# An attention block's warm-up in another order: gate matrices loaded in the prologue, first queries placed by two engines

## Chip, cores, metric

One core of a Trainium2 chip. The metric is the device time of one launch in microseconds, median of some runs; lower is better.

## The reference

A transformer block with modulation (adaLN), float32, x of 2 x 1024 x 512:

```
mod = silu(c) @ wmod                       # c 2x512, wmod 512x3072: shift, scale, gate, twice
sa, ca, ga, sb, cb, gb = mod               # gates: sign(g) * max(|g|, 0.25)
h = layernorm(x) * (1 + ca) + sa
x = x + ga * attention(h, Wq, Wk, Wv, Wo)  # 32 query heads, 8 key heads, width 64, rotary, causal
h = layernorm(x) * (1 + cb) + sb
x = x + gb * ffn(h)                        # ternary weights, silu gate, rms norm, hidden 2048
```

## The kernel before

Each engine's instructions are written out by hand; semaphores order them across engines. There are four parts: a prologue, attention, the output projection and the feed-forward part. The change is in the first two.

**Names.** TensorE is PE, VectorE DVE, ScalarE ACT, GpSimd POOL, SyncE SP. Float32 products are made of a high part (float32r) and a low part, so most tiles come in two: `hT_hi` and `hT_lo` hold the modulated, turned x, `w_hi` and `w_lo` the weights of one group (4 query heads, 1 key head, 1 value head).

**Prologue** (`prologue`). SP issues the loads: c, the first shift and scale matrices (1 MB each), x in four quarters of 512 rows, weights of group 0, rotary tables, and the second ("late") shift and scale matrices into `vectors.late[0]`. The first two quarters of x are normalised on DVE into tiles `xn`, which lie in `p_32` (`rows_at`), a tile that attention uses only later; the place for the gate matrices, `vectors.late[1]`, overlaps them. The first quarter is turned by PE and modulated by ACT. A barrier of all engines ends the prologue.

**Attention** runs in steps T = 0 to 71 for each of 8 groups g, every engine through the same `step(body, T)`. What an engine does in a step is found from tables: `body.uses(T, delay)` gives the projections that started `delay` steps ago, `body.before(T, at)` is true once, in the warm-up. The warm-up is group -1, steps 28 to 71, and does what group 0 needs before its first step. Its projections (`X_USES`) start at steps 31 and 36 (keys, with values on the upper partitions), 42 (values turned), 44, 49 (`qx`, first and last quarter of the queries' columns, two heads each), 54, 59 (`qy`, the middle quarters) and 68 (first keys of the next batch half).

A projection takes PE four steps. Then, counted from its start: at 4 DVE multiplies it with cosines and sines into `rot_c` and `rot_s` (L951, L952), which frees PSUM bank `X_BANK` for the next projection; at 5 SP swaps halves of `rot_s` into `rot_x` by DMA (L608; two transfers for keys, four for queries); at 6 POOL adds (L1051); at 8 ACT splits off the high part (queries: L907, keys: L903, at 12 in the warm-up); POOL makes the low part (queries: L1062 at 8, keys: L1056); at 10 SP places queries into `q_hl` by four DMAs (L620). There are two buffers of `rot_*`; a buffer is reused only when its placing has landed (`await_buffer`).

**Late rows and products.** The other quarters of x (n = 1, 2, 3) are finished in the warm-up: statistics (L160), square root on ACT, normalisation (L81 to L85, then four L175 into `late.xn`), PE turns (L182), ACT modulates (L853, L854, twice for each of four pieces), DVE makes the low part (L973). The first scores wait for all of ACT's modulations (`late.h_ready`), since the turns use the banks of the scores. `late_product(v)` multiplies silu(c) with the late shift, late scale and the two gate matrices (v = 0 to 3; L118, eight matrix instructions each) at steps 35, 41, 64, 66, in banks 4 and 5. The first waits for `late.h_ready` of quarter 1, because ACT still reads those banks. The gate matrices are loaded by SP at step 50. DVE makes the gates out of the last two products at steps 67 to 71, and SP stores them by eight small DMAs at step 71 (L661).

**Scores** of group 0's first rows are at steps 63 to 70 of the warm-up; DVE takes maxima (L934), ACT exponentials (L844), whose table ACT loads before the first.

Of the kernel before, what the change touches and what calls it, by code (L numbers as in the profile page):

```python
# [27 lines left out]
P = 128  # L28
B, S, E = 2, 1024, 512
T = B * S  # L30
# [62 lines left out]
class Vectors:  # L93


    def __init__(self, nc, ctx, p_32):
        sem = lambda n: ctx.enter_context(nc.semaphore("a_" + n))
        self.cs = ctx.enter_context(nc.sbuf_tensor("cs", [P, B * CT], F32))
        flat = p_32[:].rearrange("p a h c -> p (a h c)")
        size = CT * 2 * E  # L100
        self.late = [flat[:, at:at + size].rearrange("p (k v e) -> p k v e", k=CT, v=2) for at in (0, 2 * GQ * 9 * P - size)]
        self.flat = flat
# [5 lines left out]
    def rows_at(self, n):  # L108
        size = 4 * E
        return self.flat[:, (2 + n) * size:(3 + n) * size].rearrange("p (t e) -> p t e", t=4)  # L110

# [4 lines left out]
    def product(self, pe, out, wm, v):  # L116
        for kc in range(CT):
# [19 lines left out]
class LateRows:  # L137
# [11 lines left out]
    def place(self, nc, ctx):  # L149

        sb = lambda n, s: ctx.enter_context(nc.sbuf_tensor(n, s, F32))
        self.xt = sb("xt_l", [P, 2, 4, E])
        self.xn = sb("xn_l", [P, 2 * P_RING, 512])[:, 0:4, :]
        self.h32 = [sb("h32_l%d" % n, [P, 2, 512]) for n in range(2)]
# [52 lines left out]
def prologue(nc, ps, x, c, wmod, ident_in, ident, modT, hT_hi, hT_lo, vectors, late, load_first, load_tables, w_in, w_raw,  # L207
             w_hi, w_lo, k_scaled, whi_ready, w_ready):
    with ExitStack() as ctx:
# [6 lines left out]
        xt, xn = [x_rows[:, n] for n in range(2)], [vectors.rows_at(n) for n in range(2)]  # L216
# [12 lines left out]
        def _(sp):  # L229
# [14 lines left out]
            for v, place in enumerate((SHIFT[1], SCALE[1])):  # L244
                sp.dma_start(vectors.late[0][:, :, v, :], wm_v[:, :, place, :]).then_inc(vectors.late_in, 16)
            load_x(3, late.xt[:, 1])
# [135 lines left out]
def attention(nc, ps, wq, wk, wv, w_gu, w_p, consts_in, w_in, w_raw, cos, sin, mask, ident, hT_hi, hT_lo, ot_dram, rden_dram,  # L382
              tern_gu, tern_p, o_sb, o_out, load_first_weights,
              w_hi, w_lo, p_32, k_scaled, whi_ready, w_ready, vectors, late, modT, gates_dram, wmod, spare):
    with ExitStack() as ctx:
# [201 lines left out]
        def late_h32(n, k):  # L587

            return spare[:, k // 2, k % 2, :] if n == 1 else late.h32[k // 2][:, k % 2, :]


        @block.sync
        def _(sp):
# [17 lines left out]
            def place(g, n):  # L611

                kind, unit, hp, _ = X_USES[n]
                buf = buf_of(n)
                if g < 0 and kind == "qx":
                    sp.wait_ge(late.xn_ready, 3 + hp)
                q_low[buf].await_(sp, g, QBUF[buf].index(n))
                for h in range(2):
                    for at, src in ((half[0], rot_s), (half[1], rot_x)):
                        sp.dma_start(as_f32(quarters(q_hl[at, 2 * hp + h, :], kind)),  # L620
                                     src[half[h], buf, :].rearrange("p (q c) -> p q c", q=2)).then_inc(q_placed[buf], 16)

# [13 lines left out]
            def step(body, T):  # L636
                places_first = body.before(T, QUERY_SWAP)
                if places_first:
                    for g, n, _ in body.uses(T, 10, kinds=("qx", "qy")):
                        place(g, n)  # L640
                for g, n, _ in body.uses(T, 5, kinds=("kv", "qx", "qy")):
                    swap(g, n)
                if not places_first:
                    for g, n, _ in body.uses(T, 10, kinds=("qx", "qy")):
                        place(g, n)
# [28 lines left out]
        def _(pe):  # L674
# [91 lines left out]
            def late_turns(n):  # L766
                for k in range(CT):
                    if k == 0 or n == 3:
                        pe.wait_ge(late.h_ready, 2 * CT + (k + 1 if n == 3 else 0))
                    late.turn(pe, n, k, ps[:, turned_bank(n, k), :], late.xn, ident)  # L770

            def late_product(v):
                if v == 0:
                    pe.wait_ge(vectors.late_in, 32)
                    pe.wait_ge(late.h_ready, 2 * CT)
                if v >= 2:
                    pe.wait_ge(vectors.gate_in, 32)
                    pe.wait_ge(vectors.late_rows, v - 1)
                vectors.product(pe, ps[0:B, T_BANK + v % 2, :], vectors.late[v // 2], v % 2).then_inc(vectors.late_done, 1)

            def step(body, T):
# [3 lines left out]
                for v in range(4):  # L785
                    if body.before(T, LATE_AT[v]):
                        late_product(v)
# [23 lines left out]
        def _(act):  # L811
# [44 lines left out]
            def step(body, T):  # L856
# [6 lines left out]
                if body.before(T, CONSTS_AT):  # L863
                    act.wait_ge(consts_in, 48)
                    act.copy(ident_b[:], ident[:]).then_inc(consts_ready, 1)
                    act.copy(mask_b[:], mask[:]).then_inc(consts_ready, 1)
                for v in range(2):
                    if body.before(T, LATE_ROWS[v]):
                        act.wait_ge(vectors.late_done, v + 1)
                        act.copy(rd_all[0:B, v, :], ps[0:B, T_BANK + v, :]).then_inc(vectors.late_rows, 1)  # L870
# [33 lines left out]
                for g, n, _ in body.uses(T, 8, kinds=("qx", "qy")):  # L904
# [129 lines left out]
        def _(pool):  # L1034
# [4 lines left out]
            def step(body, T):  # L1039
# [18 lines left out]
                for g, n, _ in body.uses(T, 8, kinds=("qx", "qy")):  # L1058
# [727 lines left out]
```

## Time and profile before

| | |
|---|---|
| median of 3 runs | 1859.02 us (1857.18 to 1862.01) |
| profiled execution | 1858.29 us |
| its span | 1856.3 us |
| TensorE busy | 1747.3 us, 94% |
| VectorE, ScalarE, GpSimd busy | 68%, 62%, 52% |
| mean granted TensorE clock | 0.987 |

Busy shares are of the whole span. Times below are microseconds from the start of the span. In a timeline row the first number is the start and the second the length; a bracket at the end gives the idle time before the instruction and what ended it. `x4` means four instructions merged, and the length is then from the first's start to the last's end. Instructions of ScalarE and TensorE overlap their neighbours a little.

### The profile page before, as it was taken

To read this page: it belongs to the slowest core of one execution; us is meant where nothing else is said; L and a number is where in the kernel's file an instruction comes from. 1 tells how busy PE (TensorE), PEld (TensorE's weight loads), DVE (VectorE), ACT (ScalarE), POOL (GpSimd) and SP (SyncE) were. 2 spreads that over 40 slices of the span, in tenths; PEclk is the share of its full clock that TensorE was granted. 3 is DMA by queue.
4 is the path that set the end of the run, shared out by engine and by line. 5 is a ranking of instruction groups with operands and counts; after the bars stand their busy time and mean duration, and the time that the engine had idled before them with its cause. 6 is when DMAs were issued, how large, how long until landed. Compare 5 with 4: busy or idle time off the path is not lost. (4 is left out here: it accounts for less than half of the span.)

```text
span 1856.3 us, 28089 instructions
## 1 busy us (share of the span) xinstructions
PE 1747.3 (94%) x9505; PEld 1394.7 (75%) x9505; DVE 1259.0 (68%) x2078; ACT 1147.6 (62%) x2315; POOL 964.8 (52%) x773
## 2 busy tenths in 40 slices
PE   6899999999999999999999999996999999999998
PEld 3577787777777777778777777774788778888886
DVE  5787887788788778788778878884333355545343
ACT  4578787777777777877777777784322354323322
POOL 1256667666667666666766666753000035444454
PEclk9999999999999999999999999998999999999999
DMA  6433444344344344344434434425655400101000
GB/s 229 121 94 103 120 102 124 100 109 121 88 131 114 86 123 112 92 117 108 121 103 108 125 83 134 119 82 163 208 179 177 134 29 1 52 1 51 1 29 23
DMA packets 174969, 190.95 MB, mean 103 GB/s; under 512 B 31456, under 2 KB 117736, under 8 KB 174832
## 3 DMA queue, kind: packets, MB, share of 16 engines
q1 hardware_dynamic: 137840, 140.99, 26.7%
q10 hardware_dynamic: 36992, 48.25, 9.4%
q8 instruction: 72, 1.18, 0.3%
q14 instruction: 65, 0.53, 0.1%
HBM read 86.12 MB, written 31.74 MB: 63 GB/s over the span
## 5 line engine op out<-in xcount | busy, mean ns | idle before, releaser
L926 DVE TENSOR_TENSOR p_lo<-ps_b,p_hi 128x512 fp32r<-128x512 f32 x576 | 395.3, 686 | 194.7 <-ACT p_hi L829 190.8
L844 ACT ACTIVATE p<-ps_b,negm 128x640 f32<-128x640 f32 (+7 forms) x512 | 381.9, 749 | 111.4 <-DVE negm L934 108.5
L829 ACT CAST p_hi<-ps_b 128x512 fp32r<-128x512 f32 x576 | 337.0, 588 | 156.9 <-PE ps_b L748 154.2
L934 DVE TENSOR_REDUCE negm<-ps_b 128x1 f32<-128x640 f32 (+7 forms) x512 | 375.8, 744 | 34.1 <-PE ps_b L738 33.4
L748 PE MATMUL ps_b<-ident,p 128*128 128x128 f32 x2304 | 350.3, 275 | 3.1 <-DVE p_lo L926 2.1
L736 PE MATMUL ps_b<-k_hh,q_hl 128*128 128x512 f32 (+3 forms) x768 | 270.1, 352 | 37.0 <-ACT p L844 36.0
L762 PE MATMUL ps_b<-p_hi,v_hl 128*128 128x512 f32 x576 | 276.9, 481 | 16.4 <-ACT o_sb L837 16.1
L748 PEld LDWEIGHTS ps_b<-ident,p 128*128 128x128 f32 x2304 | 259.0, 141 | 37.3 <-DVE p_lo L926 5.1
L737 PE MATMUL ps_b<-k_l,q_hl 128*128 128x512 f32 (+3 forms) x768 | 256.1, 346 | 0.0
L763 PE MATMUL ps_b<-p_lo,v_hl 128*128 128x512 f32 x576 | 227.6, 395 | 0.0
L736 PEld LDWEIGHTS ps_b<-k_hh,q_hl 128*128 128x128 f32 x768 | 145.1, 189 | 87.4 <-ACT p L844 54.7
L1492 PE MATMUL ps_d<-h_hi,gu 128*128 128x512 f32 x512 | 201.0, 393 | 1.1 <-DVE h_lo L1612 1.1
L1493 PE MATMUL ps_d<-h_lo,gu 128*128 128x512 f32 x512 | 200.2, 391 | 0.0
L1042 POOL TENSOR_TENSOR o_sb<-o_sb,o_low 64x512 f32<-64x512 f32 x128 | 176.3, 1382 | 33.4 <-DMA o_low<-o_sb 33.4
L1051 POOL TENSOR_TENSOR rot_c<-rot_c,rot_x 128x512 f32<-128x512 f32 (+1 forms) x96 | 124.9, 1301 | 105.9 <-DMA rot_x<-rot_s 105.2
L700 PE MATMUL ps_b<-hT_hi,w_hi 128*128 128x512 f32 x384 | 160.4, 418 | 8.6 <-DVE rot_s L952 5.1
L1062 POOL TENSOR_TENSOR rot_x<-rot_c,rot_s 128x512 fp32r<-128x512 f32 x64 | 83.0, 1297 | 163.0 <-ACT rot_s L907 163.0
L737 PEld LDWEIGHTS ps_b<-k_l,q_hl 128*128 128x128 f32 x768 | 145.0, 189 | 27.9
L1047 POOL TENSOR_TENSOR o_sb<-o_sb,rd_all 64x512 f32<-64x512 f32 x128 | 163.4, 1281 | 3.9
L1588 POOL TENSOR_TENSOR sq<-a 128x512 f32<-128x512 f32 x60 | 71.2, 1186 | 163.9 <-DVE a L1662 163.4
L701 PE MATMUL ps_b<-hT_hi,w_lo 128*128 128x512 f32 x384 | 152.4, 397 | 0.0
L702 PE MATMUL ps_b<-hT_lo,w_hi 128*128 128x512 f32 x384 | 151.4, 394 | 0.0
(156 smaller groups left out, 3202.6 us busy)
## 6 DMA issues: line engine op xcount, KB each, us to landing
rot_x<-rot_s SPq DMA_DIRECT2D x320, 64.0 KB, 2.0
q_hl<-rot_s SPq DMA_DIRECT2D x128, 128.0 KB, 2.5
q_hl<-rot_x SPq DMA_DIRECT2D x128, 128.0 KB, 2.5
rd_all<-reciprocals SPq DMA_DIRECT2D x128, 128.0 KB, 3.0
o_low<-o_sb ACTq DMA_DIRECT2D x128, 128.0 KB, 2.4
attention_out<-o_sb SPq DMA_DIRECT2D x128, 128.0 KB, 2.5
o_raw<-attention_out SPq DMA_DIRECT2D x32, 512.0 KB, 4.9
wf<-in_L_ffn_w_gate_up ACTq DMA_DIRECT2D x32, 256.0 KB, 3.0
```

Of the source, the lines that this page charges most:

```text
L736: pe.matmul(ps[:, bank, 0:n], q, k_hh[unit][:, k0:k0 + n], start=True, stop=False)
L737: ins = pe.matmul(ps[:, bank, 0:n], q, k_l0[:, unit, k0:k0 + n], start=False, stop=(k0 + n < nk))
L748: ins = pe.transpose(ps[:, T_BANK + T % 2, h * P:(h + 1) * P], p_32[:, parity, h, column * P:(column + 1) * P], ident[:])
L762: pe.matmul(ps[:, O_BANK, :], v_hl[unit][:, j, :], p_hi[:, T % P_RING, :], start=(j == 0), stop=False)
L763: pe.matmul(ps[:, O_BANK, :], v_hl[unit][:, j, :], p_lo[:, T % P_RING, :], start=False, stop=(j == i)).then_inc(pv_done, 1)
L829: act.copy(p_hi[:, T % P_RING, :], ps[:, T_BANK + T % 2, :]).then_inc(phi_ready, 1)
L844: act.activation(p_32[:, parity, h, column * P:column * P + nk], s, ACT.Exp, bias=negm[:, k:k + 1], scale=1.0, accum_out=den[:, parity, k: ...
L926: dve.tensor_tensor(p_lo[:, T % P_RING, :], ps[:, T_BANK + T % 2, :], p_hi[:, T % P_RING, :].bitcast(F32), ALU.subtract).then_inc(plo_read ...
L934: dve.tensor_reduce(negm[:, k:k + 1], s, AX.X, ALU.max, negate=True).then_inc(max_ready, 1)
L1042: pool.tensor_tensor(o_sb[0:D, n % 2, :], o_sb[0:D, n % 2, :], o_low[:, n % 2, :], ALU.add).then_inc(o_added, 1)
L1492: pe.matmul(ps[:, bank + half, :], gu[:, m, half, k, :], h_hi[:, parity, k, :], start=(k == 0), stop=False)
L1493: i = pe.matmul(ps[:, bank + half, :], gu[:, m, half, k, :], h_lo[:, parity, k, :], start=False, stop=(k == CT - 1))
```

## The change

- `xn` of the first two quarters moves out of `p_32` into `late.h32` (now one tile) and `late.xn`. The gate matrices' place is then free in the prologue, and SP loads them there, ahead of the last quarter of x; the load at step 50 goes.
- The late products use banks 2, 3, 4, 5 and v = 0 waits for its matrices only. The second is cut in two halves, at steps 41 and 43. The turns of quarter 2 wait until ACT has copied the products out of banks 2 and 3.
- The low parts of the last two pieces of quarter 1 move from steps 33 and 34 to 36, behind the first rotation; statistics of quarter 2 from 36 to 37, its root from 41 to 38.
- `place` takes an engine and a list of heads. In the warm-up SP places head 0 of each `qx` pair at delay 10 and ACT head 1 at delay 9 (steps 53 and 58).
- In the warm-up the `qy` splits on ACT and POOL move from delay 8 to 12, their placing from 10 to 12.
- The constants' casts move from step 52 to 58, and a small exponential at step 59 has ACT load that table there.

```diff
-        xt, xn = [x_rows[:, n] for n in range(2)], [vectors.rows_at(n) for n in range(2)]
+        xt, xn = [x_rows[:, n] for n in range(2)], [late.h32, late.xn]
...
                 sp.dma_start(vectors.late[0][:, :, v, :], wm_v[:, :, place, :]).then_inc(vectors.late_in, 16)
+            vectors.load_gates(sp, wmod)
             load_x(3, late.xt[:, 1])
...
-LATE_AT, LATE_TURN, LATE_ROWS = (35, 41, 64, 66), 70, (45, 45)
-GATE_LOAD, GATE_STEPS, GATE_STORE = 50, 67, 71
-ROWS_STAT, ROWS_ROOT, ROWS_NORM, ROWS_TURN = (36, 49), (41, 50), (44, 54), (48, 58)
+LATE_AT = ((35, 0, (0, 1, 2, 3)), (41, 1, (0, 1)), (43, 1, (2, 3)), (64, 2, (0, 1, 2, 3)), (66, 3, (0, 1, 2, 3)))
+LATE_BANK, LATE_ROWS, LATE_TURN = (2, 3, T_BANK, T_BANK + 1), (45, 45), 70
+GATE_STEPS, GATE_STORE = 67, 71
+ROWS_STAT, ROWS_ROOT, ROWS_NORM, ROWS_TURN = (37, 49), (38, 50), (44, 54), (48, 58)
-ROWS_LOW = ((31, 32, 33, 34), (55, 55, 56, 56), (59, 60, 61, 62))
-CONSTS_AT, KEYS_AT, QUERY_SWAP = 52, 12, 59
+ROWS_LOW = ((31, 32, 36, 36), (55, 55, 56, 56), (59, 60, 61, 62))
+CONSTS_AT, KEYS_AT, QUERIES_AT, QUERY_SWAP, TABLE_AT = 58, 12, 12, 59, 59
...
+        def place(eng, g, n, heads):
+            kind, unit, hp, _ = X_USES[n]
+            buf = buf_of(n)
+            if g < 0 and kind == "qx":
+                eng.wait_ge(late.xn_ready, 3 + hp)
+            q_low[buf].await_(eng, g, QBUF[buf].index(n))
+            for h in heads:
+                for at, src in ((half[0], rot_s), (half[1], rot_x)):
+                    eng.dma_start(as_f32(quarters(q_hl[at, 2 * hp + h, :], kind)),
+                                  src[half[h], buf, :].rearrange("p (q c) -> p q c", q=2)).then_inc(q_placed[buf], 16)
...
+                    for g, n, _ in body.uses(T, 10, kinds=("qx",)):
+                        place(sp, g, n, (0,) if g < 0 else (0, 1))
+                for g, n, _ in body.uses(T, QUERIES_AT if body.g < 0 else 10, kinds=("qy",)):
+                    place(sp, g, n, (0, 1))
-                if body.before(T, GATE_LOAD):
-                    sp.wait_ge(vectors.late_done, 2)
-                    vectors.load_gates(sp, wmod)
...
+                    if k == 0 and n == 2:
+                        pe.wait_ge(vectors.late_rows, 2)
-            def late_product(v):
+            def late_product(v, pieces):
                 if v == 0:
                     pe.wait_ge(vectors.late_in, 32)
-                    pe.wait_ge(late.h_ready, 2 * CT)
-                if v >= 2:
+                if v >= 2 and 0 in pieces:
                     pe.wait_ge(vectors.gate_in, 32)
-                    pe.wait_ge(vectors.late_rows, v - 1)
...
+                if body.g < 0:
+                    for g, n, _ in body.uses(T, 9, kinds=("qx",)):
+                        place(act, g, n, (1,))
+                if body.before(T, TABLE_AT):
+                    act.activation(den[:, 1, :], ident[:, 0:len(ROWS)], ACT.Exp)
...
-                for g, n, _ in body.uses(T, 8, kinds=("qx", "qy")):
+                for g, n, _ in body.uses(T, 8, kinds=("qx",)) + body.uses(T, QUERIES_AT if body.g < 0 else 8, kinds=("qy",)):
```

## Rows read from the trace of the kernel before

**Rows 1.** Windows: stretch, its length, busy us by engine, clock, DMA share.
```profile
27.00:92.00 65.00, 52.55 (x218) 31.48 (x219) 43.87 (x79) 33.95 (x63) 18.05 (x14) 0.95 0.36 105
92.00:290.00 198.00, 190.21 (x1132) 153.47 (x1131) 161.57 (x272) 153.15 (x334) 125.96 (x102) 1.00 0.40 106
```

**Rows 2.** Timeline of TensorE, first key projection: start, length, line, instruction, idle.
```profile
29.75 0.39 PE L702 MATMUL ps_b<-hT_lo,w_hi 128*128 128x512 f32 x1
32.71 3.59 PE L118 MATMUL ps_b<-p,cs 128*2 128x512 f32 x8 [2.58 <-ACT hT_hi L854]
```

**Rows 3.** Timeline of VectorE, same stretch and the step after.
```profile
32.60 0.69 DVE L973 TENSOR_TENSOR hT_lo<-wo_raw,hT_hi 128x512 fp32r<-128x512 f32 x1 [0.65 <-ACT hT_hi L854]
...
45.47 1.13 DVE L85 TENSOR_TENSOR rstd<-rstd,tmp 128x4 f32<-128x4 f32 x1
```

**Rows 4.** Timeline of all engines around the value rows.
```profile
43.20 1.26 POOL L1051 TENSOR_TENSOR rot_c<-rot_c,rot_x 64x512 f32<-64x512 f32 x1 [3.88 <-DMA rot_x<-rot_s]
...
44.81 0.50 PE L700 MATMUL ps_b<-hT_hi,w_hi 128*128 128x512 f32 x1 [1.40 <-DVE v_hl L996]
...
45.27 1.31 POOL L1056 TENSOR_TENSOR k_l<-rot_c,k_hh 64x512 fp32r<-64x512 f32 x1 [0.80 <-ACT k_hh L903]
...
46.63 2.88 DVE L175 TENSOR_SCALAR xn_l<-xt_l,mv,rstd 128x512 f32<-128x512 f32 x4
```

**Rows 5.** Page, DMA issues: tiles, count, size, us to landing.
```profile
rot_x<-rot_s SPq DMA_DIRECT2D x320, 64.0 KB, 2.0
```

**Rows 6.** Timeline of SyncE, 52 to 104 us.
```profile
53.29 1.16 SPq L114 DMA_DIRECT2D p<-in_L_wmod  x2
55.80 2.42 SPq L608 DMA_DIRECT2D rot_x<-rot_s  x4
...
61.44 0.61 SPq L620 DMA_DIRECT2D q_hl<-rot_x  x1
...
91.25 1.19 SPq L608 DMA_DIRECT2D rot_x<-rot_s  x2
```

**Rows 7.** Timeline of all engines, first two groups of queries.
```profile
62.70 1.26 POOL L1051 TENSOR_TENSOR rot_c<-rot_c,rot_x 128x512 f32<-128x512 f32 x1 [3.40 <-DMA rot_x<-rot_s]
63.93 0.69 DVE L951 TENSOR_TENSOR rot_c<-ps_b,cos 128x512 f32<-128x512 f32 x1 [1.95 <-DMA q_hl<-rot_x]
63.99 0.62 ACT L907 CAST rot_s<-rot_c 128x512 fp32r<-128x512 f32 x1 [6.35 <-POOL rot_c L1051]
...
64.69 1.28 POOL L1062 TENSOR_TENSOR rot_x<-rot_c,rot_s 128x512 fp32r<-128x512 f32 x1 [0.73 <-ACT rot_s L907]
...
69.17 0.81 ACT L854 ACTIVATE hT_hi<-ps_b,modT 128x512 fp32r<-128x512 f32 x1
...
70.50 0.47 PE L736 MATMUL ps_b<-k_hh,q_hl 128*128 128x512 f32 x1 [0.63 <-DMA q_hl<-rot_x]
```

**Rows 8.** Timeline of ScalarE, the table load.
```profile
74.58 1.28 ACT L844 ACT_TABLE_LOAD   x1
75.88 1.11 ACT L844 ACTIVATE p<-ps_b,negm 128x1024 f32<-128x1024 f32 x1
...
89.31 0.19 ACT L844 ACTIVATION_READ_ACCUMULATOR p<-ps_b,negm 128x1 f32 x1
```

**Rows 9.** Timeline of ScalarE, first steps of group 0.
```profile
98.56 1.25 ACT L903 CAST k_hh<-rot_c 64x512 fp32r<-64x512 f32 x2
```

**Rows 10.** Timeline of TensorE at its next wait.
```profile
102.09 0.39 PE L736 MATMUL ps_b<-k_hh,q_hl 128*128 128x256 f32 x1 [0.97 <-ACT p L844]
```

**Rows 11.** Windows as in Rows 1.
```profile
66.00:69.00 3.00, 3.00 (x9) 2.27 (x9) 1.71 (x3) 3.00 (x5) 0.00 (x0) 0.53 0.48 114
```

**Rows 12.** Timeline of SyncE, prologue.
```profile
14.44 0.43 SPq L235 DMA_DIRECT2D xt_l<-in_L_attn_x  x1
...
16.61 2.27 SPq L235 DMA_DIRECT2D xt_l<-in_L_attn_x  x1
```

**Rows 13.** Waits of SyncE, 15 to 28 us: total, times, longest.
```profile
SPq L209 <- PEq L209: 8.0, 1, 8.0
```

More of the change, by code:

```diff
@@ L114, in load_gates, with product @@
             sp.dma_start(self.late[1][:, :, v, :], mod_columns(wmod)[:, :, GATE[v], :]).then_inc(self.gate_in, 16)
-    def product(self, pe, out, wm, v):
-        for kc in range(CT):
+    def product(self, pe, out, wm, v, pieces=range(CT)):
+        for kc in pieces:
             i = pe.matmul(out, self.cs[:].rearrange("p (b k) -> p k b", b=B)[:, kc, :], wm[:, kc, v, :],
@@ L153, in place @@
         self.xn = sb("xn_l", [P, 2 * P_RING, 512])[:, 0:4, :]
-        self.h32 = [sb("h32_l%d" % n, [P, 2, 512]) for n in range(2)]
+        self.h32 = sb("h32_l", [P, CT, 512])
     def statistics(self, dve, n, xt):
@@ L587, in late_h32 @@
         def late_h32(n, k):
-            return spare[:, k // 2, k % 2, :] if n == 1 else late.h32[k // 2][:, k % 2, :]
+            return spare[:, k // 2, k % 2, :] if n == 1 else late.h32[:, k, :]
+        def place(eng, g, n, heads):
[8 more added lines that the diff above has]
+                                  src[half[h], buf, :].rearrange("p (q c) -> p q c", q=2)).then_inc(q_placed[buf], 16)
         @block.sync
@@ L609, in swap @@
                                  rot_s[32 * (i ^ 1):32 * (i ^ 1) + 32, buf, :]).then_inc(swapped[buf], 16)
[L611 to L621, printed above, removed]
             def save_den(g, n):
@@ L643, in step @@
                 if not places_first:
-                    for g, n, _ in body.uses(T, 10, kinds=("qx", "qy")):
-                        place(g, n)
+                    for g, n, _ in body.uses(T, 10, kinds=("qx",)):
+                        place(sp, g, n, (0,) if g < 0 else (0, 1))
+                for g, n, _ in body.uses(T, QUERIES_AT if body.g < 0 else 10, kinds=("qy",)):
+                    place(sp, g, n, (0, 1))
                 for g, n in body.pairs(T, 2):
@@ L769, in late_turns @@
                         pe.wait_ge(late.h_ready, 2 * CT + (k + 1 if n == 3 else 0))
+                    if k == 0 and n == 2:
+                        pe.wait_ge(vectors.late_rows, 2)
                     late.turn(pe, n, k, ps[:, turned_bank(n, k), :], late.xn, ident)
-            def late_product(v):
+            def late_product(v, pieces):
                 if v == 0:
                     pe.wait_ge(vectors.late_in, 32)
-                    pe.wait_ge(late.h_ready, 2 * CT)
-                if v >= 2:
+                if v >= 2 and 0 in pieces:
                     pe.wait_ge(vectors.gate_in, 32)
-                    pe.wait_ge(vectors.late_rows, v - 1)
-                vectors.product(pe, ps[0:B, T_BANK + v % 2, :], vectors.late[v // 2], v % 2).then_inc(vectors.late_done, 1)
+                i = vectors.product(pe, ps[0:B, LATE_BANK[v], :], vectors.late[v // 2], v % 2, pieces)
+                if CT - 1 in pieces:
+                    i.then_inc(vectors.late_done, 1)
             def step(body, T):
@@ L784, in step @@
                         late_turns(n)
-                for v in range(4):
-                    if body.before(T, LATE_AT[v]):
-                        late_product(v)
+                for at, v, pieces in LATE_AT:
+                    if body.before(T, at):
+                        late_product(v, pieces)
                 if body.before(T, LATE_TURN):
@@ L869, in step @@
                         act.wait_ge(vectors.late_done, v + 1)
-                        act.copy(rd_all[0:B, v, :], ps[0:B, T_BANK + v, :]).then_inc(vectors.late_rows, 1)
+                        act.copy(rd_all[0:B, v, :], ps[0:B, LATE_BANK[v], :]).then_inc(vectors.late_rows, 1)
                 if body.before(T, LATE_TURN + 1):
@@ L1057, in step @@
                                        k_hh[unit][0:D, kv_cols(part)].bitcast(F32), ALU.subtract).then_inc(k_ready, 1)
-                for g, n, _ in body.uses(T, 8, kinds=("qx", "qy")):
+                for g, n, _ in body.uses(T, 8, kinds=("qx",)) + body.uses(T, QUERIES_AT if body.g < 0 else 8, kinds=("qy",)):
                     buf = buf_of(n)
```

6 lines of the change are left out of this document (removed).

## Prediction

> **What bounds the kernel now.** I read the windows first. In group 0 (92 to 290 us) TensorE is busy 190.2 of 198 us; in the stretch after the prologue (27 to 92 us) only 52.6 of 65 [rows 1]. The change touches nothing after that stretch but the order in which its leftovers are finished, so 12.4 us of idle TensorE is all there is to win, and a microsecond saved before 92 moves everything after it, since the groups are bound by TensorE. Next I read the timeline of that stretch engine by engine and, at each gap of TensorE, asked who released it. There are four gaps that matter.
>
> First, TensorE ends the first key projection at 30.14 and stands until 32.71, because the product of the late shift matrix waits for ScalarE's last modulation of rows 512 to 1023 [rows 2]. Second, after the value rows it waits for VectorE's low part and starts the first queries at 44.81; VectorE then normalises the third quarter of x until 46.63 + 2.88 = 49.51 and can only then rotate those queries [rows 4]. Third, between 53 and 64 the queries go round SyncE, GpSimd and ScalarE. The gate matrices, 2 MB, are issued at 53.29, ahead of the four swaps of the second queries (55.80); the sum that needs those swaps starts at 62.70 [rows 6, 7]. The median swap lands in 2.0 us [rows 5], so the last, issued near 57.6, would have been in at 59.7: the gates cost 3.0 us. Fourth, the scores start at 70.50, when both the last placed query and ScalarE's last modulation (69.17 + 0.81 = 69.98) are there [rows 7]. After that TensorE is nearly always busy.
>
> **The change, part by part.** I work in the old trace's times and sum the shifts.
>
> *Late products.* The shift product moves to another bank and no longer waits for ScalarE: it starts at 30.2 instead of 32.71, -2.5 us [rows 2]. The second key projection behind it also needs the low parts of that quarter. These end at 32.60 + 0.69 = 33.3 [rows 3], also when the last two go behind the first rotation; the product itself ends at 33.7, so it hides them. Of the scale product only half now stands ahead of the value rows; that is 3.59 / 2 = 1.8 us more [rows 2]. The other half runs while ScalarE and VectorE split the values, a wait TensorE has anyway. VectorE's value split thus ends at 44.75 - 4.3 = 40.5.
>
> *What is late next.* VectorE's normalisation. Of its old 4.8 us (44.75 to 49.51), L85 took 1.13 us, although it has four columns; it started at 45.47 and ended with GpSimd's L1056 (45.27 to 46.58). The four L175 behind it took 2.88 [rows 3, 4]; the second L1056 lay in them. I take about 1.9 us of the 4.8 as waiting for GpSimd. The key sum that GpSimd did at 43.20 [rows 4] now comes at 40.7 and the two key splits behind it, so the normalisation meets three of GpSimd's operations instead of two. Without any blocking it takes 2.9 us, but TensorE's query projection then ends near 44.0 and sets the rotation: -5.5. With all three in series (3 x 1.3) it takes 6.8 us: -2.2. I take one more partial wait, 5.8 us, ending 46.3: **-3.2 us**.
>
> The page "SBUF — State Buffer" of the Trainium skill, section "SBUF: two separate sides", calls the port that VectorE and GpSimd share "an exclusive lock, not a bandwidth split". The trace agrees (1.13 us for four columns). By that rule alone the three operations are all paid, and this term is -2.2.
>
> *Gates in the prologue.* Two issues go in ahead of the last load of x, which moves behind them. That load took 2.27 us to issue against 0.43 for the one before [rows 12], so issuing is already held up by the queue; two more at 2.27 end SyncE's prologue 4.5 us later. SyncE waited 8.0 us there [rows 13], which covers it. Above 4 us an issue it would not. The last quarter of x is read only near 50 us, far behind. Cost nothing; it takes away the 3.0 us delay of the second queries' swaps.
>
> *First two groups of queries.* Four placements of 0.61 us each are now split, two on SyncE, two on ScalarE; the last starts 1.2 us sooner. For the first queries this brings the third queries' rotation (63.93, held by the placing [rows 7]) forward by 1 to 2 us. But the chain that ends last goes on through ScalarE: second sum 59.7 to 61.0; split high 0.62, to 61.6; GpSimd's low split 1.28, to 62.95; ScalarE waits for this since its own placing now stands in its queue, then issues twice 0.61, to 64.2. Behind that instruction stand the four modulations of the last quarter, for which the first scores wait. They started right behind the cast of 63.99 (at about 64.5), and now at 64.2. So the 3.0 us are nearly eaten by the wait and the issues. The two small casts of constants fall in the wait for GpSimd and cost nothing; without that cover they cost under 1 us.
>
> *Table load.* It is taken from 74.58, where it held no TensorE work (the next score rows were issued meanwhile), and put between the first and second of these modulations: 1.28 us [rows 8] and some 0.2 for its small exponential. Nothing covers it there. The modulations end at 69.98 - 0.3 + 1.5 = 71.2, and the scores start at 71.2 instead of 70.50: **+0.7 us**.
>
> The page "ScalarE: Activation LUTs" of the Trainium skill, section "What ACT_TABLE_LOAD costs", gives about 1380 ns of drain on top of the load. The trace shows none: the activation starts 0.02 us behind the load. By that page the term would be +2.1.
>
> *TensorE's clock.* The fourth projection of queries now ends near 66.4 and TensorE idles until 71.2, 4.8 us. In the old trace it idled until 65.27 and in 66 to 69 us the granted clock was 0.53, the lower level of 1.2 GHz [rows 11]. That low stretch hid behind ScalarE; after 71.2 it would not. Half of 3 us is 1.5; none if the clock has risen by then. I take **+0.75**.
>
> *Third and fourth groups later.* Their splits and placements move four steps back. For the third this is free: placed before its buffer is next rotated. The fourth is now split by ScalarE behind the last warm-up exponential (ends 89.50 [rows 8]): to 90.1; GpSimd 1.28, to 91.45; SyncE places four times 0.65, to 94.05. Behind this stand the gate stores (2.4 us, until now ended at 91.2) and then the swaps of the next keys, issued at 91.25 before [rows 6] and now at 96.4. These keys are then summed from about 99.1 to 100.4. ScalarE copies them at 98.56 [rows 9] and would wait 1.8 us, with exponentials behind it; TensorE's next wait there is for just such an exponential [rows 10]. Between nothing (if ScalarE's slack takes it) and 1.9, nearer the row of a wait that is there already: **+1.5**.
>
> Sum: -3.2 + 0.7 + 0.75 + 1.5 = -0.25 us on the profiled execution's 1858.29 (1856.3 of span and 2.0 around it), so 1858.0. The median is 0.7 above that execution: 1858.8. What measurement tells from no change is 0.3%, 5.6 us.
>
> **Rivals.**
> - *Gains stand.* VectorE hardly meets GpSimd (-5.5), scores +0.7, no low clock, ScalarE's slack absorbs the late keys: -4.8, 1854.2. For it: 12.4 us of idle are there. Against: both extra waits are in plain sight. 0.20; with other small gains it passes 5.6 us in a third of these.
> - *The early gain stays with VectorE's waits.* All three of GpSimd's operations are paid in full, so the first term is -2.2, the others as above: 1859.8. For it: L85 waited for the whole rest of L1056; against: only one of the four L175 was longer, so not every operation meets one. 0.15. This is what the lock of the page "SBUF — State Buffer" would do.
> - *Slower by the clock.* After 4.8 us of idle the clock stays at 1.2 GHz through the two gate products (3.6 us each at full clock) and the score rows among them: 7.2 us and up to 2 more. It decides once the low stretch behind 71 us is over 6 us long; the one in the trace is about 3. -3.2 + 0.7 + 1.5 + 8 = +7: 1866. 0.08.
> - *The load drains.* The load holds ScalarE 1.4 us longer than its row: 1860.2. It would be a mechanism of ScalarE finishing its pending modulation before the load; a cast ends at 74.56 and the load starts at 74.58, with no such gap. The page is that of the ScalarE tables named above. 0.07.
> - *The forecast*, 1858.8, its own range 1856 to 1862: 0.50.
>
> **How the numbers follow.** All but the ends of two cases lie within 5.6 us. Faster: a third of 0.20 and a little of the others, 0.08. Slower: the clock, 0.08. Same: 0.84. For 8 in 10 the range takes in the gains case (1854.2) and the drain, and leaves out the clock case: 1853.8 to 1863.4. Its terms reach -5.5 + 0.7 at one end, and -2.2 + 2.1 + 1.5 + 1.9 = +3.3 at the other, with a microsecond for the scatter of medians.
>
> **What would show it.** In the profile after: the first late product of TensorE near 30.2; the value rows near 38.5; L175 of the third quarter ending near 46.3 (43.5 or 47.2 for the bounds); the swaps of the second queries landing 2 us behind their issue; a load of tables between two modulations; the first scores near 68.0; a clock row under 1 behind them; a ScalarE wait for GpSimd's key sum near 97 us. I am wrong if the first scores start before 66 or if TensorE shows no new idle time near 100 us, or if the gain is lost in the prologue, which should end at 27.1 as now.

## The result and the profile after

| | before | after |
|---|---|---|
| median of 12 runs | 1858.96 us | 1867.56 us |
| lowest, highest | 1855.43, 1865.49 | 1859.09, 1871.47 |
| profiled execution, span | 1858.29, 1856.3 | 1866.66, 1864.7 |
| mean granted clock | 0.987 | 0.985 |

The medians lie 8.6 us apart. The ratio, estimated from all runs, is 1.0038, 95% interval 1.0025 to 1.0050: slower by 0.38%, some 7 us (4.6 to 9.3). The forecast was 1858.8 with a range up to 1863.4 and 0.84 on "no change"; slower had 0.08.

Windows of the changed kernel, columns as in the rows before. The first two answer to [rows 1]:

```profile
27.00:92.00 65.00, 49.22 (x186) 28.21 (x186) 40.30 (x71) 30.65 (x52) 18.07 (x13) 0.87 0.30 93
92.00:290.00 198.00, 189.07 (x1110) 152.69 (x1109) 158.38 (x269) 151.77 (x333) 119.27 (x96) 0.98 0.39 103
```

TensorE did 186 instructions up to 92 us where it had done 218, at a mean clock of 0.87 instead of 0.95. To see where the time goes I measured how far each turn of probabilities in group 0 (the four transposes that open a step; L748 before, L745 after) starts behind the same one before. This is worked out from the timelines of TensorE, start minus start:

| mark | before | after | lag |
|---|---|---|---|
| first scores | 70.50 | 73.79 | +3.29 |
| turn of step 0 | 88.58 | 93.98 | +5.40 |
| step 5 | 98.53 | 103.93 | +5.40 |
| step 11 | 110.43 | 119.86 | +9.43 |
| step 0 of group 1 | 238.06 | 247.47 | +9.41 |
| last of group 7 | 1268.17 | 1277.13 | +8.96 |

All is lost in three places before 120 us: 3.3 us before the scores, 2.1 between them and step 0, 4.0 between steps 5 and 11. Then the lag stays.

The timeline of TensorE after, in the same form as [rows 2, 4, 7, 10]:

```profile
31.52 3.60 PE L113 MATMUL ps_b<-p,cs 128*2 128x512 f32 x8
...
42.27 0.50 PE L697 MATMUL ps_b<-hT_hi,w_hi 128*128 128x512 f32 x1
...
47.75 3.49 PE L177 MATMUL ps_b<-ident,xn_l 128*128 128x128 f32 x16 [2.44 <-DVE xn_l L170]
...
73.79 0.80 PE L733 MATMUL ps_b<-k_hh,q_hl 128*128 128x512 f32 x1 [7.96 <-ACT hT_hi L853]
...
75.92 4.73 PE L113 MATMUL ps_b<-p,cs 128*2 128x512 f32 x8
...
108.63 0.39 PE L733 MATMUL ps_b<-k_hh,q_hl 128*128 128x256 f32 x1 [2.11 <-ACT p L843]
```

The late product waits for nothing any more and the first queries start at 42.27 instead of 44.81. But then there is an idle stretch of 2.44 us and one of 7.96, and each time the row behind it is long: sixteen turns take 3.49 us (1.94 before), the gate product 4.73 (3.60). The clock was low in four places up to 120 us. These are the windows that TensorE worked in (the third low stretch began at 68.0, in the idle time):

```profile
27.00:30.40 3.40, 3.39 (x8) 2.72 (x9) 1.29 (x2) 3.40 (x6) 1.92 (x2) 0.51 1.05 410
47.50:50.90 3.40, 3.15 (x15) 3.19 (x16) 3.40 (x7) 2.03 (x4) 0.00 (x0) 0.50 0.15 37
73.80:78.20 4.40, 4.40 (x8) 1.65 (x9) 3.08 (x4) 0.91 (x1) 0.00 (x0) 0.50 0.13 34
109.00:115.80 6.80, 6.80 (x32) 5.54 (x31) 4.43 (x9) 3.98 (x13) 2.32 (x2) 0.50 0.09 21
```

All four are near 0.5, the lower level of 1.2 GHz, and TensorE works there nearly without a break. Each begins behind or in an idle stretch of more than 2 us: 2.96, 2.44, 7.96 and 2.11. The first of the four lies on the first key projection, which is why the late product starts at 31.52 and not near 30.2. The kernel before had its low stretches at 21.8 to 25.2, 45.7 to 49.1 and 66.2 to 69.6 us, the second 0.9 us behind an idle stretch of only 1.40 us; and it had none behind one of 2.58 us, before 32.71. So idle time alone does not tell where the clock falls.

The way to the first scores, on the timeline of the other engines (to be held against [rows 7]):

```profile
57.96 0.70 SPq L599 DMA_DIRECT2D q_hl<-rot_s  x1
...
59.06 2.49 DVE L977 TENSOR_TENSOR hT_lo<-h_l,hT_hi 128x512 fp32r<-128x512 f32 x4
...
59.65 3.03 POOL L1055 TENSOR_TENSOR rot_c<-rot_c,rot_x 128x512 f32<-128x512 f32 x1 [3.07 <-DMA rot_x<-rot_s]
...
62.71 0.62 ACT L911 CAST rot_s<-rot_c 128x512 fp32r<-128x512 f32 x1 [7.50 <-POOL rot_c L1055]
...
64.80 0.62 ACTq L599 DMA_DIRECT2D q_hl<-rot_s  x1
...
65.44 0.87 ACTq L599 DMA_DIRECT2D q_hl<-rot_x  x1
...
66.75 0.78 ACT L852 ACTIVATE h_l<-ps_b,modT 128x512 f32<-128x512 f32 x1 [3.02 <-issue]
...
68.22 1.28 ACT L870 ACT_TABLE_LOAD   x1
```

The swaps of the second queries are in by 59.65, 3 us earlier than at 62.70. GpSimd's sum then takes 3.03 us instead of 1.26: it lies over VectorE's four low parts. ScalarE casts at 62.71, and its first modulation comes 4.0 us later, at 66.75; before, it came 0.5 us behind the cast. The load of the table adds 1.5.

The third place, on the timelines of SyncE and ScalarE (against [rows 6, 9]):

```profile
98.55 2.52 SPq L658 DMA_DIRECT2D gates<-o_sb  x8
101.12 1.19 SPq L618 DMA_DIRECT2D rot_x<-rot_s  x2
```

```profile
105.10 1.26 ACT L907 CAST k_hh<-rot_c 64x512 fp32r<-64x512 f32 x2 [1.21 <-POOL rot_c L1055]
```

The next keys' swaps, 2.7 us behind the turn of step 0 before, are 7.1 us behind it now, and ScalarE waits for their sum.

### The profile page after: what moved, and what is told of

The parts are those of the page before. It is cut to its first block and busy times, and to the rows that moved or that the text cites. A ratio compares the mean times of both kernels' runs of the same rounds, so it can differ in the third digit from the quotient of the medians.

```text
span 1864.7 us, 28089 instructions
## 1 busy us (share of the span) xinstructions
PE 1748.5 (94%) x9505; PEld 1395.1 (75%) x9505; DVE 1261.1 (68%) x2078; ACT 1148.7 (62%) x2316; POOL 966.2 (52%) x773
## 5 line engine op out<-in xcount | busy, mean ns | idle before, releaser
L745 PE MATMUL ps_b<-ident,p 128*128 128x128 f32 x2304 | 351.1, 275 | 3.1 <-DVE p_lo L930 2.1
L745 PEld LDWEIGHTS ps_b<-ident,p 128*128 128x128 f32 x2304 | 259.7, 142 | 37.4 <-DVE p_lo L930 5.2
L1055 POOL TENSOR_TENSOR rot_c<-rot_c,rot_x 128x512 f32<-128x512 f32 (+1 forms) x96 | 130.1, 1356 | 116.0 <-DMA rot_x<-rot_s 115.8
L1046 POOL TENSOR_TENSOR o_sb<-o_sb,o_low 64x512 f32<-64x512 f32 x128 | 173.1, 1357 | 32.9 <-DMA o_low<-o_sb 32.8
```

Of the source, the lines that this page charges most:

```text
L745: ins = pe.transpose(ps[:, T_BANK + T % 2, h * P:(h + 1) * P], p_32[:, parity, h, column * P:(column + 1) * P], ident[:])
L1046: pool.tensor_tensor(o_sb[0:D, n % 2, :], o_sb[0:D, n % 2, :], o_low[:, n % 2, :], ALU.add).then_inc(o_added, 1)
```

## The experiments

My theory after the profiles: ScalarE's placing and the late splits of the third and fourth groups cost the most, and idle stretches cost again by the clock. The rivals are with each run. The baseline is run again beside each group of four; its median was 1858.8, 1858.0 and 1858.7 us, 35 runs each. "Under the change" compares with its median of 1867.56, which was not measured again beside them.

| run | median, us | ratio to before (95%) | first scores | lag at step 0 / step 11 |
|---|---|---|---|---|
| change | 1867.56 | 1.0038 (1.0025 to 1.0050) | 73.79 | +5.40 / +9.43 |
| a_no_table | 1864.63 | 1.0034 (1.0021 to 1.0047) | 72.35 | +4.77 / +8.77 |
| b_qy_early | 1863.18 | 1.0019 (1.0008 to 1.0031) | 73.14 | +4.71 / +5.03 |
| c_sp_places | 1862.62 | 1.0020 (1.0007 to 1.0034) | 66.74 | -2.17 / +0.21 |
| d_fill | 1861.85 | 1.0015 (1.0003 to 1.0028) | 72.47 | +2.02 / +5.24 |
| m_low_later | 1863.55 | 1.0024 (1.0012 to 1.0035) | 72.61 | +3.56 / +4.51 |
| g_gates_alone | 1859.38 | 1.0013 (1.0002 to 1.0024) | 70.50 | -0.08 / -0.12 |
| h_qy_late_alone | 1861.20 | 1.0017 (1.0007 to 1.0027) | 70.75 | +0.55 / +3.08 |
| i_act_alone | 1864.13 | 1.0030 (1.0018 to 1.0043) | 73.78 | +5.83 / +6.21 |
| j_products_alone | 1856.08 | 0.9985 (0.9972 to 0.9998) | 69.81 | -0.69 / -0.71 |
| e_sp_early | 1859.60 | 1.0003 (0.9991 to 1.0015) | 67.43 | -0.17 / -0.21 |
| f_sp_early_nt | 1856.51 | 0.9986 (0.9974 to 0.9997) | 67.98 | -2.52 / -2.53 |
| l_best_low | 1856.54 | 0.9984 (0.9972 to 0.9996) | 67.37 | -1.60 / -1.72 |

The last two columns are of one profiled execution each. It shows a mechanism, but its total is one draw of many: runs of one kernel lie 5 to 12 us apart. The start of the first late product is one such draw. Ten of these executions have the new order of the products; in six it starts at 30.3 to 30.7 us, in four (the change 31.52, a 31.59, j 32.02, m 32.04) the low clock lay on the key projection ahead of it. The four with the old order (before, g, h, i) start it at 32.6 to 32.8, in h and i too, where the projection was just as slow: there the wait for ScalarE hid it.

**a_no_table.** The change without the early load.

```diff
-                if body.before(T, TABLE_AT):
-                    act.activation(den[:, 1, :], ident[:, 0:len(ROWS)], ACT.Exp)
```

> The changed kernel without its small exponential at step 59, so that the table load goes back in front of the first exponential; the table's early load is the only thing undone. Theory (the load stands uncovered among the last modulations): the modulations of the last quarter take 5.4 us instead of 7.0, the first scores come 1.5 us earlier than after the change (72.3 instead of 73.8), the idle time of TensorE before them falls to 6.5 us, and the median is 1.5 to 2 us under the changed kernel's 1867.6. Rival (the first scores wait for the placed queries or something else, and the load only fills a wait): first scores stay at 73.8 and the time does not move.

The eight modulations of the last quarter take 5.5 us (66.84 to 72.30) instead of 7.0, and the first scores are 1.4 us earlier. So the load was on the path. The low clock behind the idle stretch ate half: the first gate product takes 5.54 us now, and step 0 is only 0.6 earlier. The median is 2.9 us lower, but the intervals overlap.

**b_qy_early.** The change with both late delays undone.

```diff
-                for g, n, _ in body.uses(T, QUERIES_AT if body.g < 0 else 10, kinds=("qy",)):
+                for g, n, _ in body.uses(T, 10, kinds=("qy",)):
...
-body.uses(T, QUERIES_AT if body.g < 0 else 8, kinds=("qy",))
+body.uses(T, 8, kinds=("qy",))
```

> The changed kernel with the third and fourth groups of queries split at delay 8 and placed at delay 10 again. Theory (the gate stores and the next keys' swaps stand behind the late placement on SyncE's queue): the swaps of the next keys are issued at 97 instead of 101, ScalarE does not wait for GpSimd's key sum near 104, TensorE's wait of 2.1 us near 106 is 1 us as before the change, and the lag that the turns of group 0 gain between step 5 and step 11 (5.4 to 9.4 us) vanishes: median 4 us under the changed kernel. Rival (that lag comes of TensorE's clock alone, which falls there in some phase of its own): the wait shrinks but the lag still grows by 2 us or more. Second rival: the splits at delay 8 hold back the first exponentials, and 1 us or so is lost at the scores.

As the theory said: the lag grows by 0.3 us between step 0 and step 11, not 4.0. The swaps go out 2.7 us behind the turn of step 0 (95.95 and 93.29), and TensorE's wait is 0.96 us as in [rows 10]. The first scores come at 73.14, 0.65 us earlier, in an execution whose late product came 0.86 earlier (30.66): the splits at delay 8 cost 0.2 us there at most.

**c_sp_places.** The change with SyncE placing both heads.

```diff
-                        place(sp, g, n, (0,) if g < 0 else (0, 1))
+                        place(sp, g, n, (0, 1))
...
-                if body.g < 0:
-                    for g, n, _ in body.uses(T, 9, kinds=("qx",)):
-                        place(act, g, n, (1,))
```

> The changed kernel with SyncE placing both heads of the first two groups of queries, ScalarE none. Theory (ScalarE's own placing makes it wait for GpSimd's low split, 1.5 us, and then issue for 1.5 us, ahead of the last four modulations): the modulations start 3 us earlier, near 63.8 instead of 66.75, the first scores come about 70.8 and then wait for modulations or for the last placing, the median is 3 us under the changed kernel, and with a shorter idle stretch up to 1 us more. Rival (placing by two engines lands the queries earlier, which is what the scores need): the last placing lands later, near 70, and nothing is gained.

More than expected in the profile: first scores at 66.74. ScalarE's timeline:

```profile
57.41 0.62 ACT L908 CAST rot_s<-rot_c 128x512 fp32r<-128x512 f32 x1 [4.19 <-POOL rot_c L1052]
...
58.34 0.77 ACT L852 ACTIVATE h_l<-ps_b,modT 128x512 f32<-128x512 f32 x1
```

The modulations follow 0.9 us behind the cast (4.0 before), and GpSimd's sum took 1.60 us here, not 3.03. Part of the 7 us is luck: in this execution the first key projection and the turns of the third quarter ran at the full clock (late product at 30.36, turns 1.94 us), which is 2.7 us of it. The median, 4.9 us under the change, is what counts. The late splits still take 2.4 us between step 0 and step 11.

**d_fill.** 34 unused matrix instructions in the idle stretch; they change no result.

```diff
+                if body.before(T, 63):
+                    for _ in range(34):
+                        pe.matmul(ps[:, O_BANK, :], w_hi[:, 0, 0:P], hT_hi[:, 0, 0:512], start=True, stop=True)
```

> The changed kernel with 34 matrix instructions of 512 columns added on TensorE between the fourth projection of queries and the first scores, into a bank that nobody reads; they compute nothing that is used, and at full clock they take 7.3 us, inside the 8.0 us of idle time. Theory (the idle stretch makes the granted clock fall, which costs 2.1 us in the first score rows and the first gate product): the gate product takes 3.6 us instead of 4.7, the first score row 1.2 us instead of 2.1, and the median is 2 us under the changed kernel. Rival (the clock has fallen for another reason, or the cost lies elsewhere): the rows behind 73.8 stay long.

```profile
64.36 7.87 PE L783 MATMUL ps_b<-hT_hi,w_hi 128*128 128x512 f32 x34
72.47 0.50 PE L733 MATMUL ps_b<-k_hh,q_hl 128*128 128x512 f32 x1 [0.25 <-ACT hT_hi L856]
...
73.66 3.60 PE L113 MATMUL ps_b<-p,cs 128*2 128x512 f32 x8
```

The score row takes 1.2 us and the product 3.60, both at full clock. From first scores to step 0 it is 18.1 us, as before the change (18.1), where the change had 20.2. So these 2.1 us are the clock's, shown by taking them away. That the scores start 1.3 us earlier than in the change is not the filler's doing: the late product came at 30.29. The median is 5.7 us under the change, more than the 2 expected. The granted clock of its twelve runs has a mean of 0.988, that of the change's twelve 0.984, and that of the kernel before beside it 0.987 to 0.988. So the filler seems to have taken away more low clock in most runs than the profile shows; where, no run shows.

**g_gates_alone.** The kernel before with the gates loaded in the prologue and the rows moved; nothing else.

```diff
+            vectors.load_gates(sp, wmod)
             load_x(3, late.xt[:, 1])
...
-                if body.before(T, GATE_LOAD):
-                    sp.wait_ge(vectors.late_done, 2)
-                    vectors.load_gates(sp, wmod)
```

> The kernel before with one part of the change: gate matrices loaded in the prologue (with the first normalised rows moved out of their place), all else as before. Theory (the gate load stood ahead of the second queries' swaps on SyncE's queue and cost them 3 us): GpSimd's second sum of queries starts near 59.7 instead of 62.7, the first scores near 67.5 instead of 70.5, median 3 us under the kernel before. Rival (prologue issues hold back the barrier, or VectorE and GpSimd meet on their operations instead): less than 1 us.

The rival's second half. The sum starts at 60.36 instead of 62.70, but:

```profile
60.22 4.63 DVE L971 TENSOR_TENSOR hT_lo<-h_l,hT_hi 128x512 fp32r<-128x512 f32 x4
64.77 0.68 DVE L949 TENSOR_TENSOR rot_c<-ps_b,cos 128x512 f32<-128x512 f32 x1
```

VectorE's four low parts, 2.5 us before, now take 4.6, since GpSimd's sum and split fall among them. The third rotation comes at 64.77 instead of 63.93, TensorE's fourth projection at 66.10 instead of 65.27, and at the low clock it ends just when the scores start, at 70.50. The low parts also began 0.7 us later than before, as the normalisation ended 0.7 us later in this run. The earlier swaps gained nothing; the median is 1.4 us over the baseline beside it, and the interval says 0.4 to 4.5 us.

**h_qy_late_alone.** The kernel before with the third and fourth groups' splits and placing at delay 12.

```diff
-                for g, n, _ in body.uses(T, 8, kinds=("qx", "qy")):
+                for g, n, _ in body.uses(T, 8, kinds=("qx",)) + body.uses(T, 12 if body.g < 0 else 8, kinds=("qy",)):
```

> The kernel before with the other suspect alone: the third and fourth groups of queries split and placed at delay 12. Theory: first scores unchanged; the next keys' swaps are issued 4.5 us later than before, ScalarE waits for GpSimd's sum near 99, and the turns of group 0 fall 1.5 to 4 us behind between step 5 and step 11; median 2 to 4 us over the kernel before. Rival (it only costs in company of the other parts, or splits out of the way of the first exponentials gain as much): same time.

```profile
100.26 1.26 ACT L905 CAST k_hh<-rot_c 64x512 fp32r<-64x512 f32 x2 [1.22 <-POOL rot_c L1053]
```

```profile
103.78 0.39 PE L738 MATMUL ps_b<-k_hh,q_hl 128*128 128x256 f32 x1 [2.11 <-ACT p L846]
```

The same 2.11 us of TensorE as in the changed kernel, and the lag grows by 2.5 us between step 0 and step 11: 1.1 at the wait, the rest behind it, where the clock was low for 3.4 us. The two runs, one that takes this part away and one that does it alone, agree.

**i_act_alone.** The kernel before with ScalarE placing head 1 of the first two groups, at delay 9.

```diff
+                if body.g < 0:
+                    for g, n, _ in body.uses(T, 9, kinds=("qx",)):
+                        place_on(act, g, n, (1,))
```

> The kernel before with one part of the change: ScalarE places head 1 of the first two groups of queries in the warm-up, SyncE head 0. Theory (ScalarE then waits for GpSimd's low split of the second queries and issues, with the last four modulations behind it): the modulations start 3 us later, near 67.5, the first scores come near 73 instead of 70.5, TensorE idles longer before them and its clock is low behind; median 3 to 5 us over the kernel before. Rival (the queries are in place earlier, so that the third rotation and the fourth projection come earlier too): the two cancel, within 1 us.

```profile
64.27 0.62 ACT L909 CAST rot_s<-rot_c 128x512 fp32r<-128x512 f32 x1 [6.40 <-POOL rot_c L1053]
...
66.32 0.62 ACTq L600 DMA_DIRECT2D q_hl<-rot_s  x1
...
68.28 0.78 ACT L852 ACTIVATE h_l<-ps_b,modT 128x512 f32<-128x512 f32 x1 [3.39 <-issue]
```

Here too 4.0 us from cast to modulation, and the first scores at 73.78, with the table load and all else as before the change. This part alone makes the kernel 5.5 us slower (3.3 to 8.0 by the interval): by the medians the largest single loss, though its interval overlaps that of h.

**j_products_alone.** The kernel before with the late products' new order and banks, and the moved low parts, statistics and root.

```diff
-LATE_AT, LATE_TURN, LATE_ROWS = (35, 41, 64, 66), 70, (45, 45)
+LATE_AT = ((35, 0, (0, 1, 2, 3)), (41, 1, (0, 1)), (43, 1, (2, 3)), (64, 2, (0, 1, 2, 3)), (66, 3, (0, 1, 2, 3)))
+LATE_BANK, LATE_ROWS, LATE_TURN = (2, 3, T_BANK, T_BANK + 1), (45, 45), 70
```

> The kernel before with one part of the change: the late products in banks 2 and 3 and in the new order, with the low parts, statistics and root moved as in the change; gates loaded at step 50 as before. Theory (VectorE's normalisation meets three of GpSimd's operations and keeps most of the gain): the value rows are turned 3 to 4 us earlier, the normalisation ends only 2 us earlier, and the chain through the swaps carries this on: median 1 to 2 us under the kernel before. Rival (all of it is lost, as TensorE then idles in another place and turns the rows at the low clock): no change.

```profile
43.27 4.72 DVE L175 TENSOR_SCALAR xn_l<-xt_l,mv,rstd 128x512 f32<-128x512 f32 x4
```

Faster, 2.6 us in the median (0.4 to 5.2). The value rows are turned at 40.30 instead of 42.70, but the normalisation takes 4.72 us for its last four instructions instead of 2.88, among three of GpSimd's. Of 2.4 us, 0.7 is left at the first scores. In this execution the clock was low on the first key projection (late product at 32.02, 1.7 us behind the best) and on the turns, which can be why the profile shows less than the median; no run separates it.

**m_low_later.** The change with VectorE's low parts of the third quarter behind the third rotation.

```diff
-ROWS_LOW = ((31, 32, 36, 36), (55, 55, 56, 56), (59, 60, 61, 62))
+ROWS_LOW = ((31, 32, 36, 36), (59, 59, 59, 59), (59, 60, 61, 62))
```

> The changed kernel with the four low parts of the third quarter moved from steps 55 and 56 to 59, behind the third queries' rotation. Theory (they are what GpSimd's sum of the second queries meets): that sum takes 1.3 to 1.6 us instead of 3.0, ScalarE's split, its placing and the modulations come 1.5 us earlier, the first scores near 72.3, median 1.5 to 2 us under the changed kernel. Rival (the sum is long because its own swaps land late): it stays at 3 us.

```profile
60.28 1.27 POOL L1055 TENSOR_TENSOR rot_c<-rot_c,rot_x 128x512 f32<-128x512 f32 x1 [3.16 <-DMA rot_x<-rot_s]
```

The sum takes 1.27 us: with nothing of VectorE's beside it, the 3.03 are gone. The scores are 1.2 us earlier, although the late product was 0.5 us later in this execution. This is the collision shown by taking it away.

The run shows one thing more, by chance. At the late keys TensorE waits 2.10 us as in the change, but the clock stays at its full level behind it:

```profile
106.79 0.38 PE L733 MATMUL ps_b<-k_hh,q_hl 128*128 128x256 f32 x1 [2.10 <-ACT p L843]
```

```profile
106.80:113.60 6.80, 6.80 (x47) 5.67 (x48) 5.91 (x13) 6.06 (x16) 2.31 (x2) 1.00 0.07 23
```

Between steps 5 and 11 the lag grows by 0.9 us here, by 4.0 in the change. So the wait costs 1 us and the low clock behind it the other 3.

**e_sp_early, f_sp_early_nt, l_best_low.** The change with c's and b's edits (e), a's too (f), and low parts at (52, 52, 55, 56) (l).

```diff
-(55, 55, 56, 56)
+(52, 52, 55, 56)
```

> The changed kernel with two parts undone: SyncE places both heads of the first two groups, and the third and fourth groups are split and placed at delays 8 and 10 again. Kept: gates in the prologue, the order of the late products, the early table load. Theory (the two losses are ScalarE's placing and the late splits, and the rest of the change gains): first scores near 67, turns of group 0 two to three us ahead of the kernel before and no new wait at steps 6 to 10; median 2 to 4 us under the kernel before, 1855 to 1857. Rival (the losses overlap, or the idle time moves to another place and the clock falls there): between the kernel before and the one with SyncE's placing alone, 1859 to 1862.

> As the run before, and the early table load undone too. Theory (once ScalarE is not made to wait, the load is covered by TensorE's fourth projection of queries, so its place no longer matters): same time as the run before within 1 us. Rival (the load stands on the path in any order): 1.5 us faster.

> The best version so far (SyncE places, third and fourth groups early, no early table load) with the low parts of the first two pieces of the third quarter moved from step 55 to 52, into VectorE's wait for the second queries' projection. Theory (GpSimd's sum of the second queries takes 3.4 us instead of 1.3 because it stands against VectorE's four low parts, which read two tiles of SBUF each): two fewer of them stand there, the sum takes at most 2.1 us, and scores and median come up to 1 us earlier, 1855.5. Rival (the length of that sum is set by something else, or the early low parts now collide with the first sum): no change.

e is as the kernel before: its first scores are 3 us earlier, but they waited 3.8 us and then the first product took 5.48 us, and all was given back by step 0. Without the early load (f) the wait is 0.95 us, the product takes 3.60, and 2.5 us are kept. So e missed its expected gain, and f's theory, that the load is covered once ScalarE doesn't wait, does not hold: e and f differ by 3 us in the median, though their intervals still overlap a little. l shortens GpSimd's sum (2.05 us against 3.38) as expected and changes the time by nothing; the projection of queries then sets the scores. f, l and j have medians 1.5 to 2.6 us below the kernel before, with intervals that end below 1.0; that is less than the 0.3% counted here as a change.

## Why the prediction was wrong

**Right.** The prologue: it ends at 27.0, so SyncE's two extra issues are covered. Late products no longer wait. The early load adds 1.5 us to the modulations (7.0 against 5.5). VectorE's normalisation became what is late next, though its end, 47.60, is beyond the bound of 47.2 that I gave (it began late, see below). The late keys hold ScalarE, by the path I described, with SyncE's queue as the cause.

**Wrong: the first scores.** Predicted +0.7 on top of -3.2, that is 68.0; measured 73.79, off by 5.8. Three steps of the prediction make it up, all in the profiled execution.
- The clock of TensorE ahead of the scores, which the sum put at nothing: +2.8. It was at 1.2 GHz over the first key projection, so that the late product started at 31.52 and not at 30.2 (+1.3), and again over the sixteen turns (+1.55). The step that I had doubted held: "one more partial wait, 5.8 us" measured 5.7, from the end of the values' split at 41.88 to the end of the normalisation at 47.60. All of it was only shifted by the slow projection. So of the early gain 0.4 us was left at the rotation of the second queries (54.12 against 54.49). I had priced the clock only behind the scores. How much of this is the change and how much the draw is open: the new order lays bare a slow key projection that ScalarE's wait used to hide, but only four of ten executions had one. And the turns can't be put down to the 2.44 us of idle before them: g idled 2.44 us before the same turns and made them at full clock, in 1.94 us.
- The step "second sum 59.7 to 61.0" kept GpSimd's old duration. Once earlier, the sum met VectorE's low parts: +1.8 us (3.03 against 1.26; m shows 1.27 without them). I had read this collision in the rows of the keys and did not ask for it again where the swaps were moved. The page "SBUF — State Buffer" of the Trainium skill, section "SBUF: two separate sides", names a VectorE operation with two SBUF inputs as one that takes the shared port; the low parts are such, and the trace agrees: 3.03 us beside them, 1.27 without.
- "then issues twice 0.61, to 64.2": from cast to modulation it took 4.04 us, not 3.2. ScalarE's two issues are 0.62 and 0.87, and 0.44 more passes before the next activation.

Gate loads out of the way were worth 3.0 us in my sum. g shows that alone they gain nothing: the swaps were hidden behind the same placing, rotation and slow projection.

**Mis-sized: the clock behind the scores.** The term was +0.75; from first scores to step 0 it measured 2.1 (d takes it away). The idle stretch was 8.0 us long, not the 4.8 I worked out, and the low stretch lasted from 68.0 to 78.2 us, not about 3; 4.4 us of it lay on work. In the six executions that idled 3.4 us or more before the scores, this part of the way took 19.5 to 21.0 us; with the clock at full behind the scores it took 18.0 to 18.1.

**Wrong: what the late groups cost.** The wait was forecast by the right path and within its bound: +1.5 taken, 1.9 at most, and 1.1 measured (2.11 us against 0.97). What the step put at nothing is the clock behind the new wait. The same wait in six executions, with b, where it is gone:

| run | TensorE's wait, us | low clock behind it, us | lag gained, steps 5 to 11 |
|---|---|---|---|
| b | 0.96 | none | 0.3 |
| m | 2.10 | none | 0.9 |
| c | 2.06 | 3.4 | 2.4 |
| h | 2.11 | 3.4 | 2.5 |
| d | 2.81 | 3.4 | 3.2 |
| a | 2.10 | 6.8 | 4.0 |
| change | 2.11 | 6.8 | 4.0 |

Sum measured: 3.3 + 2.1 + 4.0 = 9.4 us of lag, of which 0.4 to 1.0 comes back later. Low clock that the sum had at nothing or too small made 2.8 of the 5.8 us by which the first scores were missed, all of the 2.1 between them and step 0, and 3 of the 4.0 behind step 5. I named this mechanism in the slower case, but gave it one place and 0.08. That case also came near the measured time by an argument that did not happen: it had the clock low through both gate products, and only the first was slow.

The medians tell the same of the parts. Against the baseline beside each, g, h and i lose 1.4, 3.2 and 5.5 us and j gains 2.6: together 7.5 of the 8.6 us between the medians. The early table load was not run alone; taking it out of the change gave 2.9 us, which is not clear of noise.

**Open.** The scatter of one kernel's runs (12 us in the change) is larger than any term here. For the changed kernel it goes with the clock: the fastest run, 1859.09 us, had a mean granted clock of 0.987, the slowest, 1871.47 us, 0.980, and over the twelve the correlation of time and clock is -0.88. An estimate from these two: 0.007 of 1865 us is 13 us, the whole range. In the other kernels the correlation is weaker (-0.3 to -0.9). What decides whether the clock falls behind a given wait stays open, and so the change's cost has a part that is a draw in each run. g and j have medians a little off what their profiles show; that stays open too.

## What to carry to other kernels

A DMA issue on a compute engine brings its wait with it: count what stands behind it in that queue, not what it saves on the other. When a transfer is made earlier, look up what runs on the neighbour engine at the new time before keeping the old duration. And price each new idle stretch of TensorE twice: once for itself, once as a range for the instructions behind it at half the clock. Here the same wait of 2.1 us cost 0.9 to 4.0 us in all, so one profile could not have told its price.

## What the runs showed of the hardware

- A GpSimd sum of 128x512 took 1.27 us alone. Beside VectorE's four two-input operations either the sum was long (3.0 to 3.5 us) and the four took 2.5, or the sum took 1.6 to 1.7 us and the four 4.6 (c, g). VectorE had started first in both cases; what decides is not shown.
- TensorE's granted clock fell to 0.5 for 3.4, 6.8 or 10.2 us at a time, in the change behind or in idle stretches of 2.1 to 8.0 us. The same idle time did not always bring it: 2.44 us before the turns, low in the change and full in g; 2.1 us at the late keys, low in the change and h, full in m. After 7.9 us filled with unused products it was full.
- A DMA issue on ScalarE held it 0.62 to 0.87 us, and the next activation came 1.95 us behind the start of the first of two.
